# Expert loop of a one-core macaron block: outputs in two PSUM banks, turned activations in one, output copy on VectorE

## The reference, cut to what matters

```python
x = hidden_states.reshape(-1, h)                     # 4096 tokens of 128
router_logits = x @ router_w.T                       # 8 experts
top_vals, top_idx = jax.lax.top_k(router_logits, 2)
routing_weights = jax.nn.softmax(top_vals, axis=-1)
combine = jnp.sum(jax.nn.one_hot(top_idx, E) * routing_weights[..., None], axis=1)
for e in range(E):
    g = x @ gate_w[e].T                              # to 512
    u = x @ up_w[e].T
    y = jax.nn.silu(g) * u @ down_w[e].T             # back to 128
    out = out + combine[:, e:e + 1] * y
...
x = x + 0.5 * ffn(layernorm(x))
x = x + attention(layernorm(x))
x = x + 0.5 * ffn(layernorm(x))
```

## Time and profile before

| what | value |
|---|---|
| median of 3 runs | 1488.47 us (1485.82 to 1488.49) |
| the profiled execution's own time | 1478.64 us |
| its span, first to last instruction | 1476.9 us |
| first expert loop | about 78 to 303 us of the span |
| second expert loop | about 1217 to 1444 us of the span |
| busy shares of the span | PE 87%, PEld 63%, DVE 65%, ACT 53%, POOL 53% |
| mean granted TensorE clock | 0.931; in the two loops 0.99 |

### The profile page before, as it was taken

The page is one execution under the profiler, slowest core; times in us unless marked ns, Lnnn a source line. Parts: engine busy times, 40 slices in busy tenths (PEclk is TensorE's granted clock), DMA queues, the critical chain, the costliest instruction groups (busy, mean ns, idle before and its releaser), DMA issues. The chain is left out here.

```text
span 1476.9 us, 26692 instructions
## 1 busy us (share of the span) xinstructions
PE 1288.9 (87%) x8212; PEld 933.0 (63%) x8212; DVE 954.9 (65%) x2000; ACT 777.2 (53%) x2213; POOL 783.7 (53%) x726
## 2 busy tenths in 40 slices
PE   7689999922699999999999999999998959999990
PEld 7378888821366666666666666666665728888880
DVE  6833333347388888888888888888886683332334
ACT  5644444432265556565555565655655645444452
POOL 0056666532266666666656666666664015666653
PEclk7889999965599999999999999999999689999996
DMA  8011111142111221111221112221110701111115
GB/s 285 4 37 42 44 42 44 42 123 86 43 44 44 51 51 44 44 44 44 55 47 44 44 44 48 53 45 44 44 44 15 229 8 38 44 42 44 44 37 178
DMA packets 86597, 86.68 MB, mean 59 GB/s; under 512 B 10560, under 2 KB 77120, under 8 KB 85952
## 3 DMA queue, kind: packets, MB, share of 16 engines
q1 hardware_dynamic: 73024, 63.99, 16.7%
q0 software_dynamic: 9216, 18.89, 4.3%
q10 hardware_dynamic: 4224, 2.10, 0.5%
HBM read 35.66 MB, written 15.73 MB: 35 GB/s over the span
## 5 line engine op out<-in xcount | busy, mean ns | idle before, releaser
L957 POOL TENSOR_SCALAR at_prob<-at_prob,at_rec 128x128 f32<-128x128 f32 (+3 forms) x256 | 316.3, 1240 | 282.3 <-DVE at_rec L1099 282.1
L1173 ACT ACTIVATE at_prob<-at_s,at_nb 128x128 f32<-128x128 f32 (+3 forms) x512 | 265.0, 526 | 44.3 <-DVE at_nb L1091 40.4
L703 DVE TENSOR_TENSOR f_hid<-f_b,f_silu 128x512 f32<-128x512 f32 x144 | 99.6, 692 | 257.2 <-ACT f_silu L687 131.0
L1182 ACT ACTIVATE at_probT<-at_pt 128x128 f32<-128x128 f32 (+3 forms) x256 | 105.0, 436 | 261.5 <-PE at_pt L1032 261.5
L201 POOL DMA_INDIRECT f_xb<-xn_dram,f_source x144 | 139.4, 968 | 181.8 <-DVE f_source L421 126.5
L1091 DVE TENSOR_REDUCE at_nb<-at_s 128x2 f32<-128x256 f32 (+3 forms) x256 | 208.7, 816 | 16.9 <-PE at_s L1020 16.9
L593 POOL DMA_INDIRECT ys_dram<-f_y,f_target x144 | 141.8, 985 | 135.6 <-ACT f_y L683 115.0
L1085 DVE TENSOR_TENSOR at_turned<-at_pj,at_rope 128x1024 f32<-128x1024 f32 x128 | 156.2, 1220 | 54.8 <-PE at_pj L987 49.4
L1032 PE MATMUL at_pt<-ident,at_prob 128*128 128x128 f32 x1280 | 183.8, 275 | 1.8 <-DVE at_prob L1102 1.2
L1015 PE MATMUL at_s<-at_KT,at_QT 64*128 64x128 f32 (+3 forms) x1024 | 174.7, 460 | 1.4 <-ACT at_prob L1173 1.4
L639 PE MATMUL f_b<-f_down,f_hidT 128*128 x1152 | 157.9, 280 | 20.2 <-ACT f_y L683 18.9
(11 more groups left out here) (175 smaller groups left out, 2210.8 us busy)
## 6 DMA issues: line engine op xcount, KB each, us to landing
at_QT<-at_R SPq DMA_DIRECT2D x128, 128.0 KB, 2.4
at_KT<-at_R SPq DMA_DIRECT2D x128, 128.0 KB, 2.4
f_got<-ys_dram SPq DMA_DIRECT2D x32, 256.0 KB, 4.4
f_gate<-gate_t SPq DMA_DIRECT2D x16, 256.0 KB, 4.8
f_up<-up_t SPq DMA_DIRECT2D x16, 256.0 KB, 6.4
xn_dram<-f_xn SPq DMA_DIRECT2D x16, 256.0 KB, 4.6
f_down<-down_t SPq DMA_DIRECT2D x2, 2048.0 KB, 8.2
f_xb<-xn_dram,f_source POOLq DMA_INDIRECT x144
```

The source lines that it names most:

```text
L957: pool.tensor_scalar(w, w, rec[:, q, 1:2], None, ALU.mult).then_inc(probB_ready, 1)
L1173: act.activation(prob[q][:, h, :], s_bank[q % 2][:, h, 0:n], ACT.Exp, bias=nb[:, q, h:h + 1], scale=1.0, accum_out=sums[:, q, h:h + 1]).th ...
```

## The change

The two banks that held turned activations become one (bank 4), and bank 5 joins bank 7 as a second output bank. The waits follow the banks: `turn_hidden(j)` waits for the hidT copy of the block just before (`j` in place of `j - 1`), `project_down(j)` for the y copy two blocks back (`j - 1` in place of `j`). The y copy with its two waits leaves ACT's list, where it stood between the high part and silu, and enters DVE's list between the low part and the product.

```diff
-        gate_bank, up_bank, hid_bank, x_bank, y_bank = bank[0:2], bank[2:4], bank[4:6], bank[6], bank[7]
+        gate_bank, up_bank, hid_bank, x_bank, y_bank = bank[0:2], bank[2:4], bank[4], bank[6], (bank[5], bank[7])
...
                 def turn_hidden(j, k):
                     pe.wait_ge(hid_ready, j + 1)
-                    wait(pe, hidT_ready, j - 1)
+                    wait(pe, hidT_ready, j)
                     for c in range(FC):
-                        one = pe.transpose(hid_bank[k][:, c * P:(c + 1) * P], hid[k][:, c * P:(c + 1) * P],
+                        one = pe.transpose(hid_bank[:, c * P:(c + 1) * P], hid[k][:, c * P:(c + 1) * P],
                                            ident[:, :])
...
                 def project_down(j, k, e):
                     pe.wait_ge(hidT_ready, j + 1)
-                    wait(pe, y_ready, j)
+                    wait(pe, y_ready, j - 1)
                     for c in range(FC):
-                        one = pe.matmul(y_bank[:, 0:P], hidT[k][:, c, :],
+                        one = pe.matmul(y_bank[k][:, 0:P], hidT[k][:, c, :],
...
-                        act.activation(hidT[k][:, :, :], hid_bank[k][:, :].rearrange("p (c q) -> p c q", q=P),
+                        act.activation(hidT[k][:, :, :], hid_bank[:, :].rearrange("p (c q) -> p c q", q=P),
...
-                    if has(j, -3):
-                        act.wait_ge(y_psum, j - 2)
-
-                        b = (r + 1) % AHEAD
-                        wait(act, y_out[b], 16 * uses(j - 3, b))
-                        act.activation(y[b][:, :], y_bank[:, 0:P], ACT.Copy).then_inc(y_ready, 1)
...
+                    if has(j, -3):
+                        dve.wait_ge(y_psum, j - 2)
+
+                        b = (r + 1) % AHEAD
+                        wait(dve, y_out[b], 16 * uses(j - 3, b))
+                        dve.tensor_copy(y[b][:, :], y_bank[1 - k][:, 0:P]).then_inc(y_ready, 1)
                     if has(j, 0):
                         dve.wait_ge(silu_ready, j + 1)
```

## The result

| | before | after |
|---|---|---|
| median of 6 runs each | 1486.37 us (1484.98 to 1488.49) | 1495.3 us (1493.03 to 1499.49) |
| the profiled execution's own time | 1478.64 us | 1493.67 us |
| its span | 1476.9 us | 1491.9 us |
| mean granted clock | 0.931 | 0.924 |
| first L613 to last L613, loop 1 | 216.5 us | 224.2 us |

The changed kernel is slower: ratio 1.0058, 95% interval [1.0044, 1.0072], 8.9 us between the medians. I had forecast 1475.5 us, faster.

What follows compares the result with a forecast made beforehand. PE was taken to bound the kernel, at 2.84 us per block plus stalls from late signals. Profiled 1478.64 us less 13 gave 1465.6; carrying over the median's 9.8 us difference gave 1475.5 us, range 1455 to 1503.

Steps and rivals of the forecast that it cites:

- What bounds the kernel: In the two expert loops PE sets the pace, needing 2.84 us per block when it never stops.
- The ceiling: The most the two expert loops hold to gain: 433.4 us against 403.3 at 2.84 per block, 30 us.
- the late y: The y copy starts after 1.86 us idle because PE's signal comes late during POOL's train of back-to-back DMA issues.
- nothing moves: Rival, chance 0.12: an older scatter's landing delays y, or the two-block circle holds by itself; 1488.5 us.
- The y stall: PE's wait before project_down (L639) for the y copy, 18.9 us over the run, goes with the second y bank.
- The copy's prices: The y copy on DVE: 284 ns each, 41 us for both loops, at no cost to POOL's DMA issues.
- The circle: POOL's train delays PE's signals and ends waiting for one: 6.28 us per two blocks; three-block rounds at 3.01 gain 13 us.
- the 1.86: Term of the circle: us from POOL's last DMA issue of a train until PE's late signals arrive together.
- the 0.55: Term of the circle: us from the start of the y copy to POOL's next scatter.
- The single hidden bank: turn_hidden's wait for the previous hidT copy has 1.67 us of cover: 0 us, at most about 0.5 where hidT is late.
- The slow rival: Rival, chance 0.28: late signals stall PE at L613 on the low part, above 30 us; +12 us, 1500.5 us.
- The chances: Odds given: forecast 0.38, all of the stall goes 0.22, slower 0.28, nothing moves 0.12; faster by over 0.2%: 0.58.

Runs made afterwards that it cites:

- before_again: The kernel before, unchanged, profiled on a chip where it takes about 1444 us: 1444.46 against 1444.05 us, ratio 1.0005.
- scatter_c: The kernel before with only the scatters issued by SyncE as plain DMAs, on a chip where before takes 1486.46 us: 1447.05 us, ratio 0.9733.
- gather_c: The kernel before with only the gathers issued by SyncE as plain DMAs, on a chip where before takes 1486.46 us: 1445.75 us, ratio 0.9724.
- copy_only: The kernel before with only the y copy moved to DVE between low part and product, banks as before: 1487.25 against 1486.13 us, ratio 1.0009.
- banks_only: The kernel before with the banks and waits of the change, the y copy left on ACT: 1492.39 against 1486.13 us, ratio 1.0045.
- one_hidden: The kernel before with one hidden bank in place of two, y bank and ACT's list as before: 1486.27 against 1486.13 us, ratio 1.0001.
- after_again: The changed kernel again, on a chip where the kernel before takes 1444.05 us: 1441.39 us, ratio 0.9981.

## Why the prediction was wrong

**What bounds the kernel: right.** PE, at 2.84 us per block when it isn't stopped, as the kernels without holds show. The ceiling was sized a little low: 30 us, where before_again's loops are 35.1 us shorter, since a few blocks at the loop's start take 1.3 to 2.7 us.

**What the late y is: right, and now shown for the cause.** I read it as PE's signal held by POOL's train, and not as a scatter's landing. Taking either kind of issue from POOL removes it (scatter_c, gather_c), though gather_c's y copy still waits for its scatters. In the changed kernel silu and the hidT copy come late too (131.03, 133.22), and they wait for no scatter. What was not right is that the signals arrive together after the train: some arrive late within it. The rival "nothing moves" falls with it.

**The y stall goes: right.** 20.2 us before L639 became 0.4.

**The copy's prices: right.** 288 ns for an estimated 284; copy_only 1.0009, its lower end at 1.0000. The scatter issue takes 988 ns on the mean, 985 before; the 32 scatters and 43 gathers of after with a y copy beside them in time take 0.99 and 0.97 us, like the others. The Trainium skill, "SBUF — State Buffer", section "Who interferes with whom", says that a VectorE instruction with at most one SBUF input, outside the 2-port modes, does not contend with GpSimd. These rows agree.

**The circle: the step that failed.** I wrote the round as 0.55 + issues + 1.86, with the same two ends whatever its length, so that a three-block round would cost 8.86 to 9.19 us, 3.01 per block, and I gave that gain to all 108 blocks. Two terms of it, the 1.86 and the 0.55, were mis-sized for a longer train. The gap after a train of six is 3.64 us on the mean, not 2.41: in the round shown release comes 2.25 and 2.29 us after the last issue (133.22, 149.89) for 1.86, and the first scatter leaves at 134.78, 1.56 us after the release, for 0.55. I had seen that queue, the y copy behind the low part, at up to 1.75 us and put it at nothing in the forecast; with the copy on ACT (banks_only) the gap after six is still 3.31, so DVE's queue is some 0.3 us of it at most. A train of six thus costs 6.45 + 3.64 = 10.09 us, 3.36 per block. And trains of six do not follow each other: 32 of four stand between 17 of six, with a gap of 2.57 for 2.41. Of the lengths counted here, the kernel before lives on the cheapest, four at 3.14 per block; six cost 3.36, and two, in banks_only, 3.29. The evidence stood in the trace of before: its train of five, one in each loop, is followed by a gap of 3.21 and 3.20 us. In POOL's timeline of before, the next issue after the one of 264.30 is

```profile
267.51 0.98 POOL L593 DMA_INDIRECT ys_dram<-f_y,f_target  x1 [2.24 <-ACT f_y L683]
```

I measured that round from release to release, from the y copy of 257.11 to the hidT copy of 266.30, 9.19 us, and took a middle with the cheaper 8.86. That leaves out that the next scatter left 1.21 us after the release (267.51), for 0.55. From scatter to scatter, 257.67 to 267.51, it is 9.84 us, 3.28 per block: dearer than the 3.14 that it was to replace.

**The single hidden bank: right alone, wrong together.** I had 0 to 0.5 us, on 1.67 us of cover, and one_hidden gives 1.0001. In the changed kernel PE idles at L631, 17.1 us on hidT and 10.1 on the product. My reading is that the cover was there because the wait for y held PE back until the release, and that without it PE runs on to the next signal that it needs. What two hidden banks would save of the 17.1 us is not separated; the product's 10.1 us are no wait for the hidden bank.

**The slow rival: nearest, but the place was wrong.** I gave "the hold moves on, y leaves late, the next train starts late" 0.28 and 1500.5 us. Measured +8.9, forecast +12 (reach 1492 to 1506). But it moved to L631, not to L613, whose wait came to 2.3 us for the 30 that I had named as its mark. The y copy queued behind DVE's work is real in the timeline (134.22); in the sum it can't be told apart. The ratio is 1.0058 with it and 1.0045 without, and the intervals overlap.

**The chances.** What should have shifted them, as I read it now and no run tests, is that PE had only 0.5 us per pair to win while the circle was POOL's. Freeing PE's wait shortens no term of it: the release hangs on POOL's issues, and in place of 59 trains of four came 32 of four, 17 of six and 11 of two. A forecast from "who sets 6.28 us per pair" would have read "POOL and the hold", and given the freed wait nothing but risk.

**Open.** What makes a chip hold PE's signals: of the four chips of the experiments two show it and two don't, each measured at one time, with the same program at about the same clock. Why the gap is longer after a longer train: the lateness grows along the train, as the rows of the result show, but from what is not known, and the release does not follow by rule. It is later after some (2.29 us), but after the one that ends at 114.80 it came after 1.53 us, and the scatter only at 118.13. Whether the hold is in PE's signal itself or on its way to ACT and DVE: no row can tell. Whether POOL's issuing or the indirect form of the DMA does it: each run changed both. The changed kernel with fewer issues on POOL was not measured on a chip that holds; that its loss comes from the holds rests on after_again and on the count of trains. A version that is faster on both kinds of chips with the router's rows was not found; one that gathers or scatters from another engine than POOL would need indices there.

## What to carry to other kernels

Before you free an engine from a wait, ask who sets the length of the circle in which that wait stands; if it is another queue, the freed engine runs ahead and stops at the next signal, and here signals then came later, and a part of the rounds grew from two blocks to three. Price a round by the gap after trains of the length that will occur, and not by the gap after the present ones. Look whether a stall that ends "remote" exists on every chip before you tune against it: the changed kernel took 0.9981 of the time where it doesn't and 1.0058 where it does.

## What the runs showed of the hardware

The same program takes 1486 us on some chips and 1444 us on others, 2.9% apart, at a granted clock of 0.926 to 0.931 over the run. In the two profiled executions, 35.3 us apart, 35.1 us of it lie in the two loops. On the slower ones TensorE's signals reach ScalarE and VectorE 0.7 us (94.00) to 3.7 us (149.89) late while GpSimd issues indirect DMAs 1.29 us apart, later the longer the train has run; in the trace of before_again no y copy is over 0.04 us late. With one issue per block, 2.84 us apart, blocks take 2.84 us on one of the slower chips (scatter_c, gather_c) and on two of the others. One long hold of the changed kernel, PE, ACT and POOL:

```profile
112.43 0.60 PE L631 MATMUL f_b<-ident,f_hid 128*128 128x128 f32 x4
...
114.80 0.97 POOL L201 DMA_INDIRECT f_xb<-xn_dram,f_source  x1 [0.30 <-issue]
...
116.33 0.60 ACT L671 ACTIVATE f_hidT<-f_b 128x512 f32<-128x512 f32 x1 [3.03 <-remote]
```

The transposes end by the model at 113.03, and the copy that needs them starts 3.3 us later, 1.53 us after POOL's last issue.
